# Attention a tile ahead in the last tiles, and other changes of order, in a four-layer kernel on one core

## The reference

```
x = x + relu( (relu(relu(q) @ relu(k).T) / sqrt(512) + mask) @ relu(v) )   # q = ln(x) Wq + bq; k, v of the context
x = x + mxq(ln(x)) @ mxq(W).T + bias      # mxq: 6-bit grid, one scale for each block of 32
x = x + ln(x) @ W1.T + mean(ctx) @ W2.T + b
x = x + experts(ln(x))                    # 16 experts; each takes the 128 tokens of a batch with the
                                          # largest softmax (over tokens) of its gate logit ln(x) Wg + bg,
                                          # 3 layers 512x512, result times the probability, added to the tokens
```

## Time and profile before

| | us |
|---|---|
| median of 3 runs (lowest to highest) | 800.09 (799.91 to 801.5) |
| time of the profiled execution | 801.92 |
| its span | 799.9 |
| busy: PE, PEld | 706.4 (88%), 628.2 (79%) |
| busy: DVE, POOL, ACT | 576.3 (72%), 432.3 (54%), 377.5 (47%) |

### The profile page before, as it was taken

How to read it: one execution, slowest core, us unless ns; L and a number is a source line. 1 busy time by engine, 2 the same in 40 slices (tenths; PEclk the granted TensorE clock), 3 DMA queues, 4 the chain that set the end, 5 groups by cost and what they waited for, 6 DMA issues and landing times.

```text
span 799.9 us, 12388 instructions
## 1 busy us (share of the span) xinstructions
PE 706.4 (88%) x4400; PEld 628.2 (79%) x4400; DVE 576.3 (72%) x1016; ACT 377.5 (47%) x553; POOL 432.3 (54%) x589
## 2 busy tenths in 40 slices
PE   6989999999999999998887004999999999999994
PEld 6767888888888888887776003999999999999993
DVE  5785789798888978777784986476776667667751
ACT  5753354444544544333222301566556665666540
POOL 2734788887888888776663503033344433333331
PEclk9998999999999999999999556999999999999998
DMA  9610122222212221111112424387788888887642
GB/s 310 223 27 14 39 79 81 68 80 81 77 58 94 66 72 64 55 53 42 53 55 79 160 79 150 97 237 232 214 237 245 242 238 240 234 248 212 194 86 37
DMA packets 54093, 103.05 MB, mean 129 GB/s; under 512 B 5392, under 2 KB 6672, under 8 KB 54032
## 3 DMA queue, kind: packets, MB, share of 16 engines
q1 hardware_dynamic: 46864, 85.47, 32.9%
q0 software_dynamic: 7168, 16.78, 9.4%
HBM read 76.68 MB, written 25.17 MB: 127 GB/s over the span
## 4 chain that ended last, share of the span: by engine, by line
PE 69%; DVE 16%; POOL 6%; issue 4%; DMA 2%; ACT 1%; SPq 1%; POOLq 0%; DVEq 0%; ACTq 0%
PE bank L249 39%; PE banks L249 11%; PE bank L256 5%; PE banks L555 4%; PE banks L561 4%; DVE bn L1096 2%; PE banks L565 2%; PE banks L566 2%; DVE x L1272 1%; DVE pack L1356 1%; POOL xd L1591 1%; DVE left L1363 1%; DVE pos L1358 1%; DVE q L1301 1%; DMA stage<-wq 1%
## 5 line engine op out<-in xcount | busy, mean ns | idle before, releaser
L1630 POOL DMA_INDIRECT out<-y,ids x32 | 76.2, 2380 | 173.8 <-DVE y L1476 169.2
L1108 DVE TENSOR_TENSOR w_l<-w_raw,w_h 128x2048 fp32r<-128x2048 f32 x45 | 103.1, 2290 | 31.4 <-ACT w_h L844 31.4
L1059 ACT ACTIVATE h<-bank,b 128x512 f32<-128x512 f32 x64 | 44.0, 688 | 107.5 <-PE bank L249 107.5
L1096 DVE BATCH_NORM_STATS2 bn<-x 128x6 f32<-128x512 f32 x128 | 88.2, 689 | 8.2 <-DMA x<-x 4.9
L844 ACT ACTIVATE w_h<-w_raw 128x2048 fp32r<-128x2048 f32 x48 | 90.7, 1927 | 4.9 <-DMA w_raw<-w 4.9
L1108 DVE TENSOR_TENSOR hT_l<-h,hT_h 128x512 fp32r<-128x512 f32 x64 | 44.2, 691 | 67.1 <-ACT hT_h L1065 67.1
L249 PE MATMUL bank<-tokT_l,w_h 128*128 128x256 f32 x256 | 72.4, 283 | 0.0
L249 PE MATMUL bank<-tokT_h,w_l 128*128 128x256 f32 x256 | 72.4, 283 | 0.0
L249 PE MATMUL bank<-hT_h,w_h 128*128 128x256 f32 x256 | 72.4, 283 | 0.0
L249 PE MATMUL bank<-hT_h,w_l 128*128 128x256 f32 x256 | 72.4, 283 | 0.0
L249 PE MATMUL bank<-tokT_h,w_h 128*128 128x256 f32 x256 | 72.4, 283 | 0.0
(11 more groups left out here) (241 smaller groups left out, 2181.8 us busy)
## 6 DMA issues: line engine op xcount, KB each, us to landing
w_raw<-w SPq DMA_DIRECT2D x48, 1024.0 KB, 6.2
x<-x SPq DMA_DIRECT2D x32, 256.0 KB, 2.8
out<-x SPq DMA_DIRECT2D x32, 256.0 KB, 2.1
xn<-xn SPq DMA_DIRECT2D x32, 256.0 KB, 2.0
mask<-mask_t SPq DMA_DIRECT2D x8, 256.0 KB, 3.2
stage<-wk SPq DMA_DIRECT2D x1, 1024.0 KB, 8.1
stage<-wq SPq DMA_DIRECT2D x2, 512.0 KB, 8.9
stage<-wf SPq DMA_DIRECT2D x1, 1024.0 KB, 11.7
```

The lines of the kernel that those rows point to most:

```text
L1059: act.activation(h32[n % 2][:, :], ps_hid[n % 4][:, :], ACT.Relu, bias=bias)
L1096: dve.bn_stats(bn6[which][:, j % 2, :], src[:, :]).then_inc(sem_bn[which], 1)
L1108: dve.tensor_tensor(dst, src, hi_part, ALU.subtract).then_inc(sem, 1)
L1630: pool.indirect_dma_start(out=out_rows, out_offset=bass.IndirectOffsetOnAxis(ap=ids[:, r:r + 1], axis=0), in_=y[e % 2][b][:, :], in_offset ...
```

## The change

It has five parts.

1. *Attention a tile ahead.* `ahead(k)` is true for rounds 24 and later in which no scores are made. In these rounds PE runs `attend(k+1)` ahead of `t2(k)`, and DVE computes `x1(k+1)` (`first_residual`) ahead of the logit parts and `lo2(k)`. In the other rounds DVE's `x1(k+1)` stands at the end of round k, which is the place that it had at the start of round k+1.
2. *Scores' low half in two pieces.* `s_lo(g)` on POOL is one instruction over the first 128 tokens and one over the other 384; `attend` of the group's first tile waits for the first alone.
3. *Means behind the second feed-forward.* `mean_rows` moves from the end of round 1 to round 2 behind `ffn(1)`; `mean_columns`, `mean_row(0)`, `gate_shift`, and the steps of ACT and DVE that go with them move back too; `mean` on DVE moves behind `lo2(0)`.
4. *Gate product with the gate stationary.* `mix_gate` multiplies with the gate's 16 columns as stationary operand and 512 moving columns; ACT copies the 16 x 512 result (`gt`), and four small transposes (`mix_gate_turned`) bring it into the shape that it had.
5. *Smaller ones.* `t1(10)` runs behind the gate product, `norm1(10)` on ACT behind `xc(1)`, `lo1` of rounds 1 and 2 on DVE behind x2. `keep_warm` stays in round 33 alone, with four matmuls. POOL signals the inverse deviation of layer 4 (`g_r4`) before it computes the bias (`g_b4`), for which `norm(3)` waits.

```diff
+    def ahead(k):
+        return k >= N - 8 and scores_of(k) is None
...
         def attend(j):
-            pe.wait_ge(sm.s_lo, g + 1)
+            pe.wait_ge(sm.s_lo, 2 * g + (1 if j % GRP == 0 else 2))
...
         def mix_gate():
+            for o in range(C):
+                last = pe.matmul(ps_ta[0:E, :], wgf[:, o, 0:E], stage[0][:, o, :], start=(o == 0), stop=(o == C - 1))
+            last.then_inc(sm.p_set, 1)
+        def mix_gate_turned():
+            pe.wait_ge(sm.a_set, A["gt"])
             for c in range(C):
-                for o in range(C):
-                    last = pe.matmul(ps_ta[:, c * E:(c + 1) * E], stage[0][:, o, c * P:(c + 1) * P],
-                                     wgf[:, o, 0:E], start=(o == 0), stop=(o == C - 1))
+                last = pe.transpose(ps_ta[:, c * E:(c + 1) * E], gate_t[:, c * P:(c + 1) * P], ident[0:E, 0:E])
             last.then_inc(sm.p_set, 1)
...
-            if valid(k + 9):
-                t1(k + 9)
             if k == 1:
                 mix_weights(0)
                 mix_weights(1)
                 mix_gate()
             if k == 2:
-                mean_columns()
+                mean_rows()
+            if valid(k + 9):
+                t1(k + 9)
             if scores_of(k) is not None:
                 scores(scores_of(k))
             if q_units(k):
                 q_chunk(*q_units(k)[0])
-            elif valid(k - 2):
-                pe.wait_ge(sm.a_q, N)
-                keep_warm(3 if valid(k) else 6, wq_h, ps_q[0])
+            if k == 1:
+                mix_gate_turned()
             if k == 2:
-                mean_row(0)
-                gate_shift()
+                mean_columns()
+            if valid(k + 1) and ahead(k):
+                attend(k + 1)
             if valid(k):
                 t2(k)
-            if valid(k + 1):
+            if valid(k + 1) and not ahead(k):
                 attend(k + 1)
             if k == 1:
                 mix_weights(2)
                 mix_weights(3)
                 q_chunk(*q_units(k)[1])
-                mean_rows()
             if k == 2:
+                mean_row(0)
+                gate_shift()
                 mean_row(1)
...
             if valid(k - 2):
+                if k == LAST - 2:
+                    pe.wait_ge(sm.a_q, N)
+                    keep_warm(4, wq_h, ps_q[0])
                 mix(k - 2)
...
+            if k == 1:
+                norm1(10)
+                setup("wc0")
+                setup("wc1")
+                q_relu(*q_of(4))
+                setup("gt")
+            if k == 2:
+                setup("crow")
             j = k + 9
             if valid(j) and k >= 1:
                 hi1(j)
...
+        def first_residual(j):
+            dve.wait_ge(sm.p_av, j + 1)
+            dve.wait_ge(sem_x[j % XR], 16 * (j // XR + 1))
+            dve.scalar_tensor_tensor(x1[j % 2][:, :], ps_av[:, :], 0.0, x_in[j % XR][:, :], ALU.max, ALU.add)\
+                .then_inc(sm.d_x1, 1)
+            dve.wait_ge(sm.d_x1, j + 1)
+            stats(1, j, x1[j % 2], sm.d_st2)
...
+            if k in (1, 2):
+                lo1(k + 9)
...
+            if ahead(k) and valid(k + 1):
+                first_residual(k + 1)
             g = scores_of(k)
             if g is not None:
                 s_mask(g)
...
             if valid(k):
                 dve.wait_ge(sm.a_hi2, k + 1)
                 lo(sm.d_lo2, xd_l[:, :, :], in4(ps_tb), xd_h[:, :, :])
+            if k == 0:
+                setup("mean")
+            if not ahead(k) and valid(k + 1):
+                first_residual(k + 1)
             if k == 1:
+                stats1(11)
                 setup("wc2")
                 setup("wc3")
+            if k == 2:
+                setup("cg")
...
+            if which == 3:
+                inverse = r_all[1][:, j:j + 1]
+                pool.tensor_tensor(inverse, r[:, 0:1], eps_exp[:, :], ALU.pow).then_inc(sem, 1)
+                pool.wait_ge(sem, j + 1)
+                pool.tensor_scalar(r[:, 2:3], m[:, 0:1], inverse, -1.0, ALU.mult, ALU.mult).then_inc(sm.g_b4, 1)
+                return
...
         def s_lo(g):
             pool.wait_ge(sm.d_shi, g + 1)
-            lo(sm.s_lo, s_l[:, :], s32[:, :], s_h[:, :])
+            for t in (slice(0, P), slice(P, GT)):
+                lo(sm.s_lo, s_l[:, t], s32[:, t], s_h[:, t])
```

More of the change, by code:

```diff
@@ L69, in build @@
         a_xn1 a_xc a_xn4 a_hi1 a_hi2 a_hi3 a_q a_s a_l a_seg
-        g_r1 g_r2 g_r3 g_r4 g_x1b g_xd g_qlo g_x2b s_lo
+        g_r1 g_r2 g_r3 g_r4 g_b4 g_x1b g_xd g_qlo g_x2b s_lo
         k_top k_cand k_sum k_exp k_tr k_out k_pos a_soft
@@ L180, in build @@
     junk = place("mix_w_scaled", [P, C, D], at=at_ab + 4 * KB)
+    gate_t = place("mix_gate_rows", [E, D], at=at_x2 + 14 * KB)
     crow = place("mix_mean_rows", [B, D], at=at_x2 + 12 * KB)
@@ L313, in counts @@
         return at
-    A = counts("wq0 wq1 k0 k1 k2 k3 wsum v0 wf0 wf1 wf2 wf3 wcn v1 wc0 wc1 wc2 wc3 crow row0 row1")
+    A = counts("wq0 wq1 k0 k1 k2 k3 wsum v0 wf0 wf1 wf2 wf3 wcn v1 wc0 wc1 gt wc2 wc3 crow row0 row1")
     V = counts("wgc wq0 wq1 wf8 va0 v0 wf0 wf1 wf2 wf3 va1 mean wc0 wc1 v1 w1g wc2 wc3 cbcol cg")
-    T = counts("wgm k0 k1 k2 k3 v0 wf0 wf1 wf2 wf3 v1 wc0 wc1 w1g wc2 wc3 crow col row0 cg row1")
+    T = counts("wgm k0 k1 k2 k3 v0 wf0 wf1 wf2 wf3 v1 wc0 wc1 gt w1g wc2 wc3 crow col row0 cg row1")
     GS = counts("half mean k01 k23 wf")
@@ L882, in setup @@
                 last.then_inc(sm.a_set, 1)
+            if what == "gt":
+                act.wait_ge(sm.p_set, T["gt"])
+                hi(sm.a_set, gate_t[:, :], ps_ta[0:E, :])
             if what == "crow":
@@ L914, in s_relu @@
             act.wait_ge(sm.p_s, g + 1)
-            act.wait_ge(sm.s_lo, g)
+            act.wait_ge(sm.s_lo, 2 * g)
             act.activation(s32[:, :], ps_s[:, :], ACT.Relu, scale=float(D) ** -0.5).then_inc(sm.a_s, 1)
@@ L982, in _ @@
                 hi1(j)
-            if k == 1:
-                setup("wc0")
-                setup("wc1")
             j = k - 3
@@ L989, in _ @@
                     act.wait_ge(sem_xn4[j % 2], 16 * (j // 2))
-                norm(3, j, x3[j % 2], xn4[j % 2], sm.a_xn4, sm.g_r4)
+                norm(3, j, x3[j % 2], xn4[j % 2], sm.a_xn4, sm.g_b4)
             g = scores_of(k)
@@ L993, in _ @@
                 s_relu(g)
-            if k == 1:
-                q_relu(*q_of(4))
             if q_units(k):
                 q_relu(*q_units(k)[0])
-            if k == 2:
-                setup("row0")
             j = k
@@ L1006, in _ @@
                 setup("v1")
-            j = k + 10
-            if valid(j):
-                norm1(j)
             if k == 1:
@@ L1012, in _ @@
                 setup("wc3")
+            if k == 2:
+                setup("row0")
+            j = k + 10
+            if valid(j) and k >= 1:
+                norm1(j)
+            if k == 1:
                 q_relu(*q_units(k)[1])
-                setup("crow")
             if k == 2:
@@ L1198, in s_lo_first @@
             dve.wait_ge(sm.d_shi, 1)
-            lo(sm.s_lo, s_l[:, :], s32[:, :], s_h[:, :])
+            dve.tensor_tensor(s_l[:, :], s32[:, :], s_h[:, :], ALU.subtract).then_inc(sm.s_lo, 2)
         stats1(0)
@@ L1251, in logit_scale @@
                               r_all[1][:, four].unsqueeze(2).to_broadcast([P, GRP, E]), ALU.mult).then_inc(sm.d_lg, 1)
-        for k in range(LAST + 1):
[L1254 to L1262, removed]
+        def first_residual(j):
[5 more added lines that the diff above has]
+            stats(1, j, x1[j % 2], sm.d_st2)
+        first_residual(0)
+        for k in range(LAST + 1):
             j = k - 3
@@ L1307, in _ @@
                 setup("va1")
-                setup("mean")
-            if k == 2:
-                setup("cbcol")
             j = k - 2
@@ L1315, in _ @@
             j = k + 9
-            if valid(j) and k >= 1:
+            if valid(j) and k >= 3:
                 lo1(j)
@@ L1330, in _ @@
                 setup("w1g")
+            if k == 2:
+                setup("cbcol")
+            if ahead(k) and valid(k + 1):
+                first_residual(k + 1)
             g = scores_of(k)
@@ L1334, in _ @@
             j = k + 10
-            if valid(j) and k >= 1:
-                dve.wait_ge(sem_x[j % XR], 16 * (j // XR + 1))
-                stats(0, j, x_in[j % XR], sm.d_st1)
+            if valid(j) and k >= 2:
+                stats1(j)
             if parts_of(k) is not None:
                 logit_parts(parts_of(k))
-            if k == 2:
-                setup("cg")
             if valid(k):
@@ L1515, in rstd_of @@
                 return
-            inverse = r_all[1][:, j:j + 1] if which == 3 else r[:, 1:2]
-            then(pool.tensor_tensor(inverse, r[:, 0:1], eps_exp[:, :], ALU.pow))
+            if which == 3:
[4 more added lines that the diff above has]
+                return
+            then(pool.tensor_tensor(r[:, 1:2], r[:, 0:1], eps_exp[:, :], ALU.pow))
```

(2 more changed lines are left out.)

## The result

The changed kernel takes 786.37 us (median of 4 runs, 785.45 to 786.94) beside 800.00 us (799.36 to 801.50) of the kernel before on the same chip: 0.9826 of it, 95% interval 0.9809 to 0.9843. Timed again later it took 785.58 beside 799.77: 0.9820 [0.9806, 0.9835]. The forecast was 787.0. The profiled execution took 786.94 us with a span of 785.1.

What follows compares the result with a forecast made beforehand. PE was taken to set the pace in the first 438 us, with a ring through DVE, POOL and PE in the last rounds. From the median 800.1, -4.3 -3.75 -5.0 = -13.1 gave 787.0 us; range 782.5 to 793.

Steps and rivals of the forecast that it cites:

- behind the narrow product the clock fell: Round 1: the 16-column gate product lets the clock fall to 0.50, the wide form keeps it; -2.54 and -0.31 us.
- the 2.85: Round 1: gain in us from the kept clock, 2.54 on the query chunk and 0.31 on the transposes of `t2(1)`.
- The wait of 0.46 in `t2(1)`: First rounds: new wait of 0.46 us for `lo1(10)`, which now stands behind `x2(0)` and its statistics on DVE.
- The wait of 0.45 before `mix(0)`: First rounds: new wait of 0.45 us, as `gate_shift` comes last and DVE copies `cg` only behind `first_residual(3)`.
- The earlier `ffn(0)`: First rounds: with `mean` no longer ahead of `lo2(0)` on DVE, `ffn(0)` starts 0.6 us earlier.
- The wait of 1.76: Round 1: PE's stop for `norm1(10)`, expected to be covered by the new order; -1.76 us.
- the clock falls in round 1 all the same: Rival for round 1: small transposes still lower the clock, 2.85 us are lost, 789.9 us; chance 0.12.
- `s_lo` in two pieces: Rounds with scores: each group's first `attend` released 0.75 us sooner, five groups -3.75 us, plus part of round 27.
- Round 26 and 27: Last rounds: `mix_bias(25)` starts earlier, `logit_scale` meets POOL less (-0.6), the shorter first piece gives 0.75; together -1.35 us.
- The turns: Rounds 28 to 30, a ring through DVE, POOL, PE: `attend` leaves it, -0.70 us in 28 and 29, -0.3 in 30.
- the cold case: Rival for the last rounds: without `keep_warm` the clock stays at 0.5 from round 27 on, 814 us; chance 0.03.
- a dip less in the last rounds: Rival: a clock dip behind `attend(28)` or `t2(31)` goes, 1.5 us each, 784 to 785.5 us; chance 0.2.

Runs made afterwards that it cites:

- third look: The kernel before, unchanged, traced a third time to look at its clock in round 1; 798.09 us.
- narrow_gate: The changed kernel with the old gate product (32 matmuls of 16 columns, no `gt`, no small transposes); 787.26 us, 0.9833 of the kernel before.
- one_piece: The changed kernel with `s_lo` as one instruction over 512 tokens again; 792.60 us, 0.9891 of the kernel before.
- before_again: The kernel before, unchanged, run once more for a second trace; 797.97 us.
- wide_gate_only: The kernel before with only the gate product changed: gate stationary, its copy and its transposes; 800.43 us, 1.0000 of the kernel before.
- not_ahead: The changed kernel with `ahead` false in every round, `keep_warm` of the last rounds still removed; 792.77 us, 0.9894 of the kernel before.
- not_ahead_warm: The changed kernel with `ahead` false and the old `keep_warm` back in rounds 27 to 32; 791.96 us, 0.9902 of the kernel before.

## Why the prediction was right, and where it wasn't

The total came out (787.0 for 786.37) with one step not borne out, and in part by luck. Below are the stretches between marks that every trace has, in us: the trace of before that the prediction rests on, the third look at it, and after. x3(25) is the one of round 27.

| stretch | before | before, third look | after | gain on the first, on the third | predicted |
|---|---|---|---|---|---|
| `attend(0)` to `attend(4)` | 57.29 | 54.10 | 52.41 | 4.9, 1.7 | 4.3 |
| to `attend(24)` | 230.12 | 230.18 | 226.03 | 4.1, 4.15 | 3.75 |
| to `attend(28)` | 44.51 | 44.49 | 42.98 | 1.5, 1.5 | 1.35 |
| to x3(25) | 5.65 | 5.54 | 5.66 | 0, -0.1 | 0 |
| to x3(28), three turns | 28.82 | 28.81 | 26.69 | 2.1, 2.1 | 1.7 |
| to x3(29) | 11.65 | 11.67 | 10.92 | 0.7, 0.75 | 0.6 |
| to x3(30) | 7.56 | 7.54 | 6.18 | 1.4, 1.4 | 1.36 |
| to the top-k stage | 11.9 | 11.90 | 11.95 | 0, 0 | 0 |

**The step that failed: "behind the narrow product the clock fell".** The row was there, and the product stood in front of it, but the one didn't follow from the other each time: behind the narrow product the clock was 1.00 in two further traces of before and in narrow_gate. Without the 2.85 the forecast of these rounds was 1.45. Measured against the third look is 1.7, and 0.4 of it belongs to the pieces (52.80 in one_piece, 52.42 after), which the prediction put at nil for the first group; 1.3 is left.

Its parts are others than the sum had. The product doesn't give back 0.04 but costs 0.41, since its 3.90 was already slowed. The wait of 0.46 in `t2(1)` was real, as narrow_gate shows, but the four transposes stand in it. The wait of 0.45 before `mix(0)` didn't come; one of 0.18 before `t2(2)` did. The earlier `ffn(0)` gave about 0.4 and not 0.6: from `attend(0)` to the gate product it is 16.02 us in before_again and 13.18 after, and 1.76 and the 0.66 of the moved transposes are taken off. The wait of 1.76 is gone, as forecast: -1.76 +0.41 +0.18 -0.4 is -1.6 for the measured -1.3, and the rest is open. Taken as a whole, the new gate product is worth at most 0.9 us (787.26 against 786.37, with overlapping intervals), and nothing from `attend(0)` to `attend(4)`: 52.31 in narrow_gate, 52.42 after. No run takes back the moved means and the other changes of order alone, so the 1.3 us rest on these readings.

Yet the step was not wholly wrong, by what the clocks on record suggest. The span times the missing share of the mean clock, doubled, is the time that an execution had at half clock. This is an estimate, since the mean clock is given to three digits. It is 73 us in the two traces of before without the dip (796.0 us at 0.954) and 79 in the one with it (799.9 at 0.951). For the median of the timed executions of before, 798.0 us at 0.952, it is 76.6: some 3.4 us more at half clock, which costs 1.7 where TensorE is busy throughout, in a span that is 2.0 longer. Of the 31 timed executions of before 26 were under 0.954, of the ten of wide_gate_only none. So the wide form, or the shift in time that comes with it, probably does spare the kernel a fallen stretch in most executions, shorter than the one of the first trace. That it stands in round 1 was seen in one trace alone, and one_piece shows another place where the half clock can last 3.4 us longer; narrow_gate, with four executions at 0.952 to 0.954 beside nine of the changed kernel at 0.952 to 0.957, doesn't decide it. The link stays open. The rival "the clock falls in round 1 all the same" is not what happened either: in no trace of the changed kernel did it fall there.

**Why the total held nevertheless.** It was made from the median, 800.1, with a gain that was read against a trace of 801.9 with the dip. Against that trace the change gains 15.0 us (801.92 to 786.94); against the other two, 11.0 and 11.2 (797.97 and 798.09). The median of before lies between. Over 31 timed executions its span ran from 795.9 to 800.0 us; the five with a mean clock of 0.950 or 0.951, as the trace with the dip has, took 799.2 to 800.0, the five with 0.954 took 795.9 to 798.4. In sum: the stretches give 11.4 where 10.25 was forecast without the 2.85; the rest of the kernel took 0.3 back; the median of before lies 2.0 above its two executions without the dip, and that of after 0.5 below its profiled ones. 11.1 + 2.0 + 0.5 is the 13.6 of the medians. Where the forecast had 2.85, there came 2.5 from the spread of the executions and 1.2 less 0.3 from the rest. That these came to nearly the same was luck, except for that part of the 2.0 which may be clock that the change gives back.

**`s_lo` in two pieces** was right in mechanism and placed a little low: 0.80 to 0.82 a group instead of 0.75, since the first piece takes 0.451 us where the line through two rows gave 0.51, and the wait for it nearly vanished. The group of `attend(4)`, put at nil, gave another 0.4: there TensorE comes to `attend` 0.69 us behind the start of the transposes before it in before_again, 0.35 after. The upper bound of 4.4, "all of these waits", should have been 4.2 (7.4 less the 3.2 of round 27). No rival held here: POOL's and DVE's queues took the longer work without a loss.

**Round 26 and 27.** `mix_bias(25)` did start ahead of `logit_scale`, whose 1.21 us became 0.40. By the queues' order 0.6 was taken, by the Trainium skill (SBUF — State Buffer, Who interferes with whom) 0.95; one_piece, which has the order without the pieces, shows 0.71 for rounds 24 to 27, between the two; not_ahead, which has the pieces without the order, lacks the same 0.70 (43.68 against 42.98). The trace agrees with that page as far as it goes: 0.26 us of overlap is left, and with it `logit_scale` takes 0.13 more than its shortest, 0.271.

**The turns** of rounds 28 and 29 gave the 0.70 each that `attend` takes, and round 30 the same 0.70, not 0.3: DVE, said to bound it with its logit parts, did not. The statement that TensorE would be "idle about 0.6 instead of 1.4" was wrong: the wait is 1.34. Of the two reasons given against the cold case only the first was left, that waits of 1.36 didn't lower the clock. From x3 to `t2` it is 5.2 us in both kernels, and `attend` fills of it what the three fillers had filled, 0.7 us each: the sum had counted the fillers as if they took no time in the wait.

**The dips** stayed, as taken, for about the reason given: in round 27 the wait got shorter (3.18 to 2.29) but emptier. The cost was read right, 1.5 us. The rival "a dip less in the last rounds" needed work in these waits; with three matmuls in each it came true. "The last rounds run cold" had its mechanism confirmed, in a kernel that isn't the changed one: without both `attend` and fillers rounds 28 and 29 fell to 0.50, for some 3 us each and not throughout, at 1.5 us a round. The Trainium skill (TensorE: Matmul & The Clock Gate, Why this matters for your kernels) names idle gaps between bursts as what drops the clock; the runs agree in part, as shown above: 1.36 idle never, 2.04 in two of three. The fillers of the kernel before had an effect: they held the clock in rounds 28 to 30, and `attend` took that over.

## What to carry to other kernels

A clock dip in one trace is not yet the kernel's: look at a second execution before giving its price to an edit, compare the mean clocks of the timed ones, and take the sum from a trace whose events are all in the runs that the median is of. Real work moved into a wait does two things, it leaves the ring and it holds the clock; when fillers are taken out, count the idle time that is left in each wait and put three of them back where it passes what the traces show to be safe (1.7 us here), and never straight on the chain. A producer of one tile that several rounds read can be cut so that the first reader waits for its part alone; what that gives is the difference in duration, as long as the next bound is some tenths away.

## What the runs showed of the hardware

The same code ran with a dip to 0.50 in round 1 in one trace of three, and with dips in rounds 27 and 31 in all three. Idle stretches of TensorE of 1.3 to 1.7 us were never followed by a fall in these rounds. Of those of 2.0 us and more most were: 3.18 and 2.46 in before, 2.29 and 2.38 after, 2.43, 2.03 and 2.04 in not_ahead, 2.46 in not_ahead_warm; but another 2.04 and 3.17 in not_ahead, and 2.36 behind three fillers in not_ahead_warm, were not. The length of the last idle stretch alone doesn't decide it, and what does stays open. A dip of round 27 or 31 cost 1.55 us: it lasted 3.4 us at 0.50, with TensorE busy for nearly all of it. The clock at the start of the experts came back 6.1 us behind TensorE's first matmul in one execution (after) and 9.6 behind in another (one_piece).

32 f32 matmuls of 16 moving columns took 3.48 us at full clock, and eight of 512 columns for the same product 3.54.
